# A recurrent block on TensorE: r's two products of each step as four products of 32 output columns instead of two of 64

## The reference, cut to what matters

```python
def step(carry, inp):
    h_ssm, h_rnn = carry
    bxt, dxt, gxt, iht = inp
    h_ssm = jax.nn.silu(h_ssm @ A.T + bxt)
    y_ssm = h_ssm @ Cw.T + Cb + dxt
    hh = h_rnn @ W_hh.T + b_hh
    i_r, i_z, i_n = jnp.split(iht, 3, axis=-1)
    h_r, h_z, h_n = jnp.split(hh, 3, axis=-1)
    r = jax.nn.sigmoid(i_r + h_r)
    z = jax.nn.sigmoid(i_z + h_z)
    n = jnp.tanh(i_n + r * h_n)
    h_rnn = (1.0 - z) * n + z * h_rnn
    y_rnn = h_rnn @ proj_w.T + proj_b
    fused = gxt[:, :1] * y_ssm + gxt[:, 1:2] * y_rnn
    return ((h_ssm, h_rnn), fused)
```

## Time and profile before

| what | value |
|---|---|
| median of 3 runs | 695.53 us (695.49 to 697.72) |
| the profiled execution's own time | 697.02 us |
| its span in the profile | 695.2 us |
| granted TensorE clock | 0.999 of full speed |
| busy: PE, PEld, DVE, ACT, POOL | 684.6, 641.9, 533.8, 429.5, 121.0 us |
| instructions | 35722, of them 13868 multiplies and 13868 weight loads |

### The profile page before, as it was taken

One profiled execution on the slowest core, in us unless ns is written; L12 is line 12 of the kernel. 1 busy time (PEld: TensorE's weight loads), 2 busy tenths in 40 slices (PEclk: granted clock), 3 DMA queues, 4 the chain that ended last, 5 costly groups with the idle time before them and its releaser, 6 DMA issues.

```text
span 695.2 us, 35722 instructions
## 1 busy us (share of the span) xinstructions
PE 684.6 (98%) x13868; PEld 641.9 (92%) x13868; DVE 533.8 (77%) x3216; ACT 429.5 (62%) x2688; POOL 121.0 (17%) x209
## 2 busy tenths in 40 slices
PE   7999999999999999999999999999999999999997
PEld 5899999989999999999999999999999999998896
DVE  4777777777887777887887788878877888875666
ACT  4555555556666666557666775676666676666442
POOL 4011111111011111112112211121212212221202
PEclk9999999999999999999999999999999999999999
DMA  8916000603522100044322000642210163323431
GB/s 309 364 61 220 8 7 7 223 33 133 183 94 86 53 15 15 14 168 175 126 86 71 22 15 19 215 163 95 94 61 23 56 230 117 110 67 93 154 102 55
DMA packets 45658, 71.97 MB, mean 104 GB/s; under 512 B 6156, under 2 KB 28498, under 8 KB 45362
## 3 DMA queue, kind: packets, MB, share of 16 engines
q1 hardware_dynamic: 41490, 64.38, 26.3%
q0 software_dynamic: 1984, 4.07, 2.0%
q10 hardware_dynamic: 2016, 1.25, 0.6%
HBM read 14.31 MB, written 21.04 MB: 51 GB/s over the span
## 4 chain that ended last, share of the span: by engine, by line
PE 97%; DVE 1%; issue 0%; ACT 0%; DVEq 0%
PE rs_bank L1223 34%; PE nz_bank L1223 24%; PE hid_bank_b L1223 12%; PE work L1223 11%; PE y_bank L1223 9%; PE hid_bank_a L1223 7%; DVE fin_g L1199 0%; DVE acc L1157 0%; DVE o_sb L1204 0%; DVE hid_b L1179 0%; ACT xT L783 0%; ACT hid_a L790 0%; DVE prob L1023 0%; DVE y_sb L1193 0%; DVE fin_g L1211 0%
## 5 line engine op out<-in xcount | busy, mean ns | idle before, releaser
L1223 PE MATMUL nz_bank<-h_ring,wg 128*64 128x16 f32 x4088 | 207.2, 211 | 0.0
L798 ACT ACTIVATE r_fac<-rs_bank 128x8 f32<-128x8 f32 x512 | 91.6, 179 | 169.0 <-PE rs_bank L1223 161.8
L1223 PE MATMUL rs_bank<-s_ring,ws_sb 128*64 128x128 f32 x1024 | 195.1, 272 | 0.0
L1223 PEld LDWEIGHTS nz_bank<-h_ring,wg 128*64 128x64 f32 x4088 | 160.8, 136 | 1.4
L1223 PE MATMUL rs_bank<-mw,wg 128*64 128x8 f32 x2044 | 146.8, 202 | 0.0
L1223 PE MATMUL rs_bank<-u,wg 128*64 128x8 f32 x2044 | 140.6, 206 | 0.1
L1223 PEld LDWEIGHTS rs_bank<-s_ring,ws_sb 128*64 128x64 f32 x1024 | 127.2, 136 | 9.1
L1104 DVE TENSOR_TENSOR_SCAN nz_bank<-r_fac,nz_bank 128x16 f32<-128x16 f32 x512 | 99.7, 195 | 46.3 <-ACT r_fac L798 30.8
L1108 DVE SCALAR_TENSOR_TENSOR mw<-v_fac,h_ring 128x8 f32<-128x8 f32 x512 | 85.7, 167 | 57.5
L1223 PEld LDWEIGHTS rs_bank<-mw,wg 128*64 128x64 f32 x2044 | 103.4, 135 | 18.8 <-DVE mw L1108 4.6
L804 ACT ACTIVATE v_fac<-nz_bank 128x8 f32<-128x8 f32 x512 | 91.1, 178 | 42.0
(11 more groups left out here) (181 smaller groups left out, 1125.0 us busy)
## 6 DMA issues: line engine op xcount, KB each, us to landing
wx<-w_all SPq DMA_DIRECT2D x58, 578.0 KB, 3.5
rows<-zeros SPq DMA_DIRECT2D x3, 4096.0 KB, 14.5
rows<-y_sb SPq DMA_DIRECT2D x66, 64.0 KB, 1.8
w_all<-in_w SPq DMA_DIRECT2D x2, 2048.0 KB, 15.1
xs_sb<-rows SPq DMA_DIRECT2D x54, 64.0 KB, 2.9
x_sb<-in_x SPq DMA_DIRECT2D x1, 1920.0 KB, 7.4
out<-o_sb SPq DMA_DIRECT2D x19, 64.0 KB, 2.6
out<-o_sb ACTq DMA_DIRECT2D x13, 64.0 KB, 1.7
```

Source lines behind the costliest of these rows:

```text
L798: nc.scalar.activation(r_fac[:, k, :, 1], r_cols(q, t), ACT.Tanh, scale=0.5).then_inc(rn_ready, 1)
L1223: last = nc.tensor.matmul(out[c:c + COLS], weights[:, c:c + COLS], moving, start=start, stop=stop, skip_group_check=skip_group_check)
```

## The change

`mm` takes the block width as an argument `cols`, with 64 as its default. The two products that make r, of mw in `carried` and of u in `step`, pass 32. So each of these two products is four matmuls of 32 weight columns instead of two of 64, in each of the steps; their sum is the same, the semaphore increment still hangs on the last. Nothing else differs.

```diff
 COLS = 64
+R_COLS = 32
...
-            def mm(out, weights, moving, start, stop, skip_group_check=False):
-
-                for c in range(0, weights.shape[1], COLS):
-                    last = nc.tensor.matmul(out[c:c + COLS], weights[:, c:c + COLS], moving, start=start, stop=stop,
+            def mm(out, weights, moving, start, stop, skip_group_check=False, cols=COLS):
+
+                for c in range(0, weights.shape[1], cols):
+                    last = nc.tensor.matmul(out[c:c + cols], weights[:, c:c + cols], moving, start=start, stop=stop,
                                             skip_group_check=skip_group_check)
                 return last
...
-                mm(r_cols(q, t), wg[:, WG_M:WG_M + P], mw[:, (g - 1) % 2, :], start=False, stop=True, skip_group_check=True)
+                mm(r_cols(q, t), wg[:, WG_M:WG_M + P], mw[:, (g - 1) % 2, :], start=False, stop=True, skip_group_check=True,
+                   cols=R_COLS)
...
                     mm(r_cols(q, t), wg[:, WG_R:WG_R + P] if g else w_sb[:, W_HH:W_HH + P], u[:, k, :],
-                       start=False, stop=True, skip_group_check=True).then_inc(r_ready, 1)
+                       start=False, stop=True, skip_group_check=True, cols=R_COLS).then_inc(r_ready, 1)
```

## The result

The changed kernel is slower: 738.46 us against 695.51, medians of 4 runs each; ratio 1.0625, 95% interval 1.0603 to 1.0647. The profiled execution took 736.45 us with a span of 734.6, 39.4 more than the span before. Ratios in this document compare the fast runs alone (within 1.5% of the fastest of their kernel); medians are over all runs.

The account below looks back on a forecast made before the run. Bound by the latency of the loop from u to u. Gain 0.004 us a step over 511 steps is 2.0: 697.02 - 2.0 = 695.0 us, 693.5 on the median's scale; 8-in-10 range 688.5 to 725.

Parts of the forecast that it names:

- The ring: From u through its product, r_fac, scan and n_fac to the next u: 1.21 us without slack, bounding the kernel.
- the second ring through h: Path from u through h and n's product to the scan, n ready at 302.10; untouched by the change.
- the tie at the scan: Paths through r_fac and n both reach the scan at 302.10, within 10 ns; n's slack nothing to 0.014 us.
- The u product: Product of u for r, 0.34 us of the step; claimed 0.014 to 0.04 us earlier with 32 columns.
- The halving of the load: Weight load in u's product: assumed to shrink from 0.055 us at 64 columns to 0.028 at 32.
- two drains: TensorE waits at the two width changes a step; claimed hidden unless together over 0.13 us.
- that sum: TensorE's own work in the heavy step: 0.83 + 0.11 + 0.06 + 0.08, making 1.08 of 1.21 us.
- Rival 1: Each width change drains the array to the modelled multiply ends, up to +0.22 us a step: 777 us; chance 0.30.
- some 11 us: Cost of short drains at the width changes: 0.15 us together, +0.02 a step, 706 us.
- a stated rule against the change: Trainium skill's rule that changing the tiling mode drains TensorE; no time given, no row shows or excludes it.
- the likeliest case: The forecast itself: a small gain limited by n at the scan, range 688.5 to 696 us; chance 0.37.
- More instructions ... I take nothing: Eight more load and multiply pairs a step, 33 in 1.21 us: issuing them claimed no bound, cost nothing.

Follow-up runs that it names:

- s64_after: The changed kernel with 64 instead of 128 moving columns in the state-space product; 746.45 us, ratio 1.0546.
- all32: Every product of the kernel in blocks of 32 columns, so the width never changes; 889.04 us, ratio 1.2752 to the kernel before.
- mw32: The changed kernel with u's product back at 64 columns, mw's stays at 32; 753.71 us.
- u32: The changed kernel with mw's product back at 64 columns, u's stays at 32; 734.37 us.
- ssm32: The kernel before with the state-space product alone at 32 columns, r at 64; 781.72 us.
- r128: The changed kernel with each of r's products as one block of 128 columns; 880.98 us.
- pieces: The kernel before with each filling product of 256 moving columns issued as three of 88, 84 and 84; 700.97 us, ratio 1.0083.
- late32: The changed kernel with r's products at 64 columns in the first 64 steps, 32 from the 65th; 725.04 us, ratio 1.0404.
- late_both: The kernel before up to step 95; from step 96 r's products at 32 columns and the state-space product at 64 moving columns; 699.0 us, ratio 1.0035.
- halfhold: The changed kernel with its 256-column filling products cut to 128 columns; 743.03 us, ratio 1.0662.

## Why the prediction was wrong

- **The reading of before holds.** The ring, the second ring through h, and the tie at the scan stand: in s64_after the scan waits for n and the step is 1.20 us, near the forecast's 1.208 - 0.004. all32, where both paths are shorter, has 1.18.
- **The u product** is shorter in the way that I worked out: u's first load to r_fac is 0.33 instead of 0.34 in the changed kernel, and 302.06 - 301.75 = 0.31 in s64_after, where no load queues behind mw's. There r_fac starts 0.37 after u's end, inside the forecast's 0.35 to 0.375. The halving of the load, then an assumption, fits: the shortest load takes 0.105 us with 32 columns, 0.132 with 64 and 0.186 with 128, so 32 columns are 0.027.
- **The step that failed first is the chance given to the change of width.** I wrote that two drains "must exceed 0.13 together to decide anything; below that they are hidden, and the forecast stands", and took that as the likeliest. They are 0.20 + 0.11 after the last multiply's start. Counted as in that sum: 0.83 to the last state-space multiply, 0.20 to mw's load, 0.06 to u's, 0.08 for u, 0.10 to 0.11 to n's load: 1.27 to 1.28 us, the usual step measured. In that sum's own terms: it had 0.11 for the last state-space multiply's columns and nothing behind u's, where 0.20 and 0.11 stand; so the drains are 0.20 together, 0.07 more than the 0.13 of room, and 1.21 becomes 1.28. Rival 1's mechanism and its ring were right. Its two prices were off: the drain doesn't run to the modelled end of the multiply (301.33 and 301.58 against 301.40 and 301.65), and "some 11 us" for a short one was the smallest of many. By the trace of before, nothing between 0 and 0.22 a step could be excluded; with a stated rule against the change and nothing but a few ns for it, the likeliest case should have been the loss.
- The Trainium skill, "TensorEngine Tiling (Array Packing)", Key Properties: changing the mode, and not only the tile, drains TensorE. By that rule the trace agrees, in all the timelines read for it (the changed kernel, mw32, u32, ssm32, r128), though not up to the modelled ends: the next load starts 0.20 behind a 128-column float32 multiply, 0.10 to 0.18 behind one of 8 columns, against 0.06 where the width stays.
- **The second step that failed is "More instructions ... I take nothing".** I compared 33 pairs a step with how closely four can start, which is how fast the engine takes instructions that it has. How fast they arrive is another number, and no row of before was starved. It is worth 4 to 9 us of the 43: pieces is +5.1, the stalls of the changed kernel's trace add up to 6.8, and late32 gives back 8.4 (spans) to 13.4 (medians), of which 64 x 0.063 = 4 are held-back loads.
- The expected gain, 2 us, is real where the holds are covered, and smaller than the stalls that come with it (late_both).

The sum as it should have been, for the two profiled executions: 447 x 0.063 = 28, 64 x 0.063 = 4, stalls 7: 39 of the 39.4 us. The 0.063 is read from r_fac; the holds give 0.06 to 0.07 by the sum above. The medians lie 43 us apart only because the profiled execution of before was 1.5 us above its median and that of the changed kernel 2.0 below.

What stays open: why the hold behind an 8-column product is 0.10 after 32 columns, 0.13 after 64 and 0.18 after 128 (the steps of 0.03 and 0.05 are those of a load's length, but u and mw products differ in other ways too), and what exactly the early stalls wait for. They are more frequent before 80 us, when the DMA engines are half busy (share 0.55 between 12 and 80 us of the changed kernel, against 0.22 to 0.25 later), but no run separates this from the early place in the program.

## What to carry to other kernels

Before you give one product of a tight loop its own column width, count the changes of width that it brings: here each put the next load 0.1 to 0.2 us behind the start of the last multiply, and was free only where TensorE had that much room and nothing latency-bound stood right behind it. Splitting a product into narrower blocks shortens its latency (here by 0.01 to 0.03 us) but doubles its instructions, and a stream of small matmuls can run out of instructions long before it runs out of array: check the "issue" waits, and instructions per microsecond against what the same program has ever kept up. And filling work that looks useless can be what holds the clock, as in halfhold: try a cut on its own and read the granted clock by slices.

## What the runs showed that I had not expected

- TensorE got about 64 instructions a microsecond in all32, and the stalls came at whole multiples of 252 to 256 instructions (163 of 165 distances), in the few stalls of pieces and of the changed kernel too. The kernel before, at 41 a microsecond, had next to none; the changed kernel, at about 52 (2 x 33 in 1.28 us), had a few, most of them early.
- In float32, a load of 64 columns holds up the next one for 0.055, of 32 for under 0.03, of 128 for 0.11; the bf16 load of 64 took 0.03. So time goes with columns and with the type.
- Halving the moving columns of the state-space product (0.11 us less for its columns a step) took the granted clock from full to 1.2 GHz for some 70 to 90 us of the early steps (s64_after), while the same edit on the kernel before (s64_before) left it at 1.00 and gave 0.3%. Why the changed kernel alone lost it is not shown.
